# A two-layer 3x3 convolution with group norm: from 64x64 tiles on overlapping bands, two images at a time, to dense blocks of 16 rows by 8 channels, one image at a time, in 64x32 and 32x32 tiles

## The chip, the cores and the metric

The kernel runs on one core of one Trainium2 chip, alone. The metric is the device time of one execution in microseconds; lower is better. All arithmetic is float32.

## The reference

```python
def _gn(v, G=4, eps=1e-5):
    g = v.reshape(B_, G, C_ // G, H_, W_)
    m = jnp.mean(g, axis=(2, 3, 4), keepdims=True)
    s = jnp.var(g, axis=(2, 3, 4), keepdims=True)
    return ((g - m) / jnp.sqrt(s + eps)).reshape(v.shape)

# x: (8, 8, 1024, 1024) float32; each conv is 3x3, 8 to 8 channels, stride 1, padding 1, plus bias
x = x + _L0_conv_ref(_gn(x), L0_conv_weight, L0_conv_bias)
x = x + _L1_conv_ref(_gn(x), L1_conv_weight, L1_conv_bias)
return x
```

Group norm is over 2 channels of one image (4 groups). One image is 33.5 MB and x is 268.4 MB, so nothing stays on the chip between the layers. The normalisation is folded into the weights (scaled by 1/std) and the bias, the border is padded with the mean, and the residual is an identity added to the middle tap. Layer 0's result goes to a tensor mid in device memory, in the order row, channel, column.

## The kernel before

**Windows.** The images go in four pairs. A window is one layer of one pair; eight windows run in the order L0 pair 0, L0 pair 1, L1 pair 0, L0 pair 2, L1 pair 1, L0 pair 3, L1 pair 2, L1 pair 3 (WINDOWS). Statistics of x for a later pair are taken while a window runs: 4 or 8 tiles of 1 MB per 8 units; the last three windows have none.

**Units.** A unit is 12 output rows of both images, as two bands: 8 input rows by 8 channels (64 partitions) make 6 output rows by 8 channels (48 columns of a 64-column tile). Neighbouring bands share 2 input rows. There are 85 units and a short last one in a window, 688 in all. `convolve` (matmul at L653) does a unit in two halves of 512 columns, three horizontal taps kw each, and for each of these six steps four matmuls of 64x64, one for each quarter of the array. In layer 0 every band's 8 rows are read from x; in layer 1 the rows of mid are read once and the shared rows are copied on chip, by POOL (L405) and by ACT (L508).

**Engines.** SP issues the statistics loads. ACT evicts (L465 both images in layer 0, L470 one band in layer 1) and then issues the loads of the unit 8 ahead (L479, L492). DVE takes statistics of x (L700) and mid (L710), and in layer 1 evicts the second band (L727). POOL issues the stores (L371, L385). x_tile has a ring of 8 units, out_tile one of 4, the accumulator conv two halves used in turn. TensorE waits only at fixed places ahead of the next unit: for its rows, halos and accumulator.

**Sums.** The mean and variance of the next window are combined by small 128x128 matmuls (L555, L564), DVE steps (L746 to L828) and bias matmuls (L583, L592), all put among the last units of the window, so that TensorE's stream goes on between them. Only before the first window do they stand alone.

## Time and profile before

| | |
|---|---|
| runs | 4156.16, 4156.9 and 4147.31 us, median 4156.16 |
| span of the profiled execution | 4141.6 us, first to last instruction |
| TensorE matmul | 89% busy, 33232 records |
| DVE, ACT, POOL | 49%, 43%, 33% busy |
| device memory | 895.64 MB read, 536.87 MB written |

The span leaves out what lies around it in a run, so the timed runs are a little longer. A busy TensorE in this table means that at least one matmul is in its modelled length, not that the array is full. Each float32 matmul of the program stands as two records.

### The profile page before, as it was taken

To read this page: it belongs to the slowest core of one execution; us is meant where nothing else is said; L and a number is where in the kernel's file an instruction comes from. 1 tells how busy PE (TensorE), PEld (TensorE's weight loads), DVE (VectorE), ACT (ScalarE), POOL (GpSimd) and SP (SyncE) were. 2 spreads that over 40 slices of the span, in tenths; PEclk is the share of its full clock that TensorE was granted. 3 is DMA by queue.
4 is the path that set the end of the run, shared out by engine and by line. 5 is a ranking of instruction groups with operands and counts; after the bars stand their busy time and mean duration, and the time that the engine had idled before them with its cause. 6 is when DMAs were issued, how large, how long until landed. Compare 5 with 4: busy or idle time off the path is not lost.

```text
span 4141.6 us, 88712 instructions
## 1 busy us (share of the span) xinstructions
PE 3666.7 (89%) x33232; PEld 1715.4 (41%) x33232; DVE 2025.6 (49%) x3110; ACT 1762.8 (43%) x1381; POOL 1360.0 (33%) x1829
## 2 busy tenths in 40 slices
PE   0087777898889999999888999999999999999999
PEld 0032222353334433354333443345444444566665
DVE  6866666665556344446656444444445322232222
ACT  0032222343334555543333555544443555555554
POOL 0011111121112555531111455552111455555555
PEclk9999998999999999999999999999999999999999
DMA  9989999999999999999999999999999999999997
GB/s 333 396 291 393 386 374 371 366 368 387 382 382 331 331 367 385 380 318 391 390 388 384 305 357 371 374 295 368 362 355 333 291 306 306 306 287 304 305 303 237
DMA packets 367109, 1435.04 MB, mean 346 GB/s; under 512 B 49888, under 2 KB 50016, under 8 KB 334176
## 3 DMA queue, kind: packets, MB, share of 16 engines
q10 hardware_dynamic: 176736, 627.30, 47.9%
q0 software_dynamic: 153344, 536.96, 34.5%
q1 hardware_dynamic: 36864, 268.45, 16.9%
q8 instruction: 119, 1.95, 0.2%
q14 instruction: 46, 0.38, 0.0%
HBM read 895.64 MB, written 536.87 MB: 346 GB/s over the span
## 4 chain that ended last, share of the span: by engine, by line
PE 56%; DMA 15%; ACTq 11%; issue 10%; DVE 5%; ACT 2%; DVEq 0%; POOL 0%; POOLq 0%; SPq 0%
PE conv L653 56%; DMA out_dram<-out_tile 12%; ACTq L479 11%; DMA stat_tile<-x_dram 2%; DVE bn_x L700 2%; ACT out_tile L465 1%; DVE bn_mid L710 1%; DMA mid_dram<-out_tile 1%; DVE out_tile L727 1%; DVE mv_mid L738 1%; DVEq L700 0%; DVE mv_x L732 0%; PE conv L555 0%; ACTq L461 0%; PE conv L583 0%
## 5 line engine op out<-in xcount | busy, mean ns | idle before, releaser
L653 PE MATMUL conv<-x_tile,wts 64*64 64x512 f32 x32832 | 3648.7, 598 | 235.5 <-ACT out_tile L465 140.4
L653 PEld LDWEIGHTS conv<-x_tile,wts 64*64 64x64 f32 x32832 | 1694.9, 134 | 2170.3 <-issue 2037.0
L465 ACT ACTIVATE out_tile<-conv,bias 128x1024 f32<-128x1024 f32 x688 | 728.6, 1110 | 1340.5 <-PE conv L653 791.1
L710 DVE BATCH_NORM_STATS2 bn_mid<-out_tile 128x512 f32 (+1 forms) x1376 | 849.3, 680 | 881.1 <-ACT out_tile L465 880.9
L727 DVE TENSOR_SCALAR out_tile<-conv,bias 128x1024 f32<-128x1024 f32 x340 | 436.4, 1284 | 1168.7 <-PE conv L653 856.7
L371 POOL DMA_DIRECT2D mid_dram<-out_tile x680 | 343.4, 507 | 1708.1 <-ACT out_tile L465 1641.4
L470 ACT ACTIVATE out_tile<-conv,bias 128x1024 f32<-128x1024 f32 x344 | 383.1, 1114 | 764.4 <-PE conv L653 505.6
L508 ACT ACTIVATE x_tile<-x_tile 16x2048 f32<-16x2048 f32 x340 | 648.6, 1908 | 44.9 <-issue 31.6
L700 DVE BATCH_NORM_STATS2 bn_x<-stat_tile 128x512 f32 (+1 forms) x1024 | 628.7, 678 | 45.6 <-DMA stat_tile<-x_dram 45.5
L405 POOL COPY x_tile<-x_tile 16x2048 f32<-16x2048 f32 x340 | 639.1, 1880 | 1.7
L385 POOL DMA_DIRECT2D out_dram<-out_tile x680 | 348.3, 514 | 823.7 <-DVE out_tile L727 758.8
L555 PE MATMUL conv<-share,average 128*128 128x8 f32 x32 | 5.5, 281 | 227.4 <-DVE share L746 222.3
L555 PEld LDWEIGHTS conv<-share,average 128*128 128x128 f32 x32 | 4.8, 215 | 233.3 <-issue 221.5
L396 POOL COPY x_tile<-pad 128x4 f32<-128x4 f32 x64 | 12.2, 198 | 173.2 <-DVE pad L821 172.1
L522 ACT ACTIVATE root<-var 128x8 f32<-128x8 f32 x8 | 1.7, 208 | 137.3 <-DVE var L790 137.2
L738 DVE BATCH_NORM_AGGREGATE mv_mid<-bn_mid 128x2 f32<-128x12 f32 (+1 forms) x24 | 40.1, 1698 | 0.0
L522 ACT ACT_TABLE_LOAD x1 | 1.3, 1283 | 84.5 <-issue 84.5
L732 DVE BATCH_NORM_AGGREGATE mv_x<-bn_x 128x2 f32<-128x192 f32 x32 | 29.9, 983 | 0.0
L335 POOL TENSOR_SCALAR own_group<-same_group 128x4 f32<-128x4 f32 x2 | 0.4, 188 | 44.0 <-DMA rows<-taps_dram 43.9
L379 POOL DMA_DIRECT2D out_dram<-out_tile x16 | 7.8, 495 | 13.4 <-ACT out_tile L470 13.4
L592 PEld LDWEIGHTS conv<-taken,band 64*64 64x64 f32 x144 | 7.2, 134 | 2.2 <-issue 2.2
L583 PE MATMUL conv<-taken,band 64*64 64x1 f32 x144 | 5.5, 208 | 2.7 <-DVE taken L818 2.7
(62 smaller groups left out, 114.5 us busy)
## 6 DMA issues: line engine op xcount, KB each, us to landing
x_tile<-x_dram ACTq DMA_DIRECT2D x680, 512.0 KB, 23.0
stat_tile<-x_dram SPq DMA_DIRECT2D x256, 1024.0 KB, 9.8
out_dram<-out_tile POOLq DMA_DIRECT2D x680, 384.0 KB, 7.8
mid_dram<-out_tile POOLq DMA_DIRECT2D x672, 384.0 KB, 9.3
x_tile<-mid_dram ACTq DMA_DIRECT2D x340, 640.0 KB, 6.4
x_tile<-mid_dram ACTq DMA_DIRECT2D x344, 128.0 KB, 8.5
mid_dram<-out_tile POOLq DMA_DIRECT2D x8, 416.0 KB, 10.0
x_tile<-x_dram ACTq DMA_DIRECT2D x8, 256.0 KB
```

The lines of the kernel that those rows point to most:

```text
L371: pool.dma_start(mid[win.image + i, bass.ds(unit.n * OUT_ROWS + (CH - extra), OUT_ROWS + extra), :], out_tile[VALID - extra:VALID + OUT_RO ...
L385: pool.dma_start(pair[:, bass.ds(row, ROWS_OUT), :], out_tile[VALID:VALID + OUT_ROWS, slot, band]) \
L405: pool.tensor_copy(x_tile[0:PAIR, unit.slot, :, 1:SIDE + 1], x_tile[HALF:HALF + PAIR, earlier.slot, :, 1:SIDE + 1]) \
L465: last = act.activation(out_tile[0:parts, slot, i], conv[0:parts, bank, i], ACT.Identity, bias=bias0[0:parts, win.parity, int(unit.last), ...
L470: last = act.activation(out_tile[:, slot, 0], conv[:, bank, 0], ACT.Identity, bias=bias1[:, win.parity, unit.kind:unit.kind + 1])
L479: act.dma_start(x_tile[:, slot, band, 1:SIDE + 1], rows.rearrange("n c r w -> (n c) r w")) \
L508: act.activation(x_tile[HALF + HALF // 2:HALF + HALF // 2 + PAIR, unit.slot, :, 1:SIDE + 1], x_tile[HALF // 2:HALF // 2 + PAIR, unit.slot, ...
L653: last = nc.tensor.matmul(to, weights, x_tile[HALF * half:HALF * (half + 1), slot, middle, c + kw:c + kw + BANK], start=(kw == 0), stop=(k ...
L700: last = dve.bn_stats(bn_x[:, bass.ds(t * STAT_PARTS + q, 1), :].rearrange("p a b -> p (a b)"), stat_tile[:, s, q * BANK:(q + 1) * BANK])
L710: last = dve.bn_stats(bn_mid[0:parts, unit.win.pair % 2, i, bass.ds(unit.n * 2 + h, 1), :] .rearrange("p a b -> p (a b)"), out_tile[0:part ...
L727: dve.tensor_scalar(out_tile[:, slot, 1], conv[:, bank, 1], bias1[:, win.parity, INNER:INNER + 1], None, ALU.add) \
L738: return dve.bn_aggr(mv_mid[:, region, i, :], bn_mid[:, of.pair % 2, i, first:end, :] .rearrange("p a b -> p (a b)"))
```

## The change

The bands go. A block is 16 rows by 8 channels of one image, 128 partitions with nothing twice; block b of x_tile holds input rows 16b+1 to 16b+16, so that the output rows 16b to 16b+15 need its 15 first rows, its last for the row below, and the last two rows of the block before. A unit is two blocks (32 rows), 32 units are a pass, and a pass is one layer of one image: 16 passes in the order image 0 layer 0, image 0 layer 1, image 1 layer 0 and so on. Output rows come in quarters of 4 rows by 8 channels (32 columns). Quarters 1 and 3 need rows of one half of the block alone: `whole`, a 64x32 matmul. Quarters 0 and 2 need 32 partitions of their own and 32 above: `split`, two 32x32 matmuls. In the second block of a unit the quarters are shifted by two column strips, so that the four whole tiles cover strips 1 and 3 and the eight split tiles strips 0 and 2. Eviction swaps the halves back (three ACT operations). The part above adds into the other column half's bank, and a wait (half_added) keeps the two halves of a unit's split tiles apart.

All loads are issued by SP, up to seven blocks ahead; all evictions are ACT's; POOL issues the stores. The sums of a pass stand between passes: `sums` on TensorE comes after the last convolution and before the next, and layer 1's need the statistics of all of mid. Statistics tiles of the next image (32) go along units 0 to 58, with two extra at units 31 and 33. TensorE runs in a loop over passes with a loop over trips of four units inside.

```diff
-ROWS_IN = 8
-ROWS_OUT = 6
-BANDS = 2
+BLOCKS = SIDE // ROWS
+UNITS = BLOCKS // 2
+TRIP = 4
+TRIPS = UNITS // TRIP
+SLOTS = 2 * TRIP
+PASSES = 2 * IMAGES
+RING = 4
+EVICTS = 3
+FREE = 6
+STAT_UNITS = sorted(list(range(0, 60, 2)) + [31, 33])
+STAT_AHEAD = 2
...
+    x_by_row = x.rearrange("n c h w -> h n c w")
+    out_by_row = out.rearrange("n c h w -> h n c w")
...
-        x_tile = sb("x_tile", [P, X_RING, BANDS, SIDE + 2])
+        x_tile = sb("x_tile", [P, SLOTS, SIDE + 2])
...
+            def load_block(layer, n, b):
+                first = ROWS * b + 1
+                rows = ROWS - 1 if b == BLOCKS - 1 else ROWS
+                sp.dma_start(x_tile[0:CH * rows, b % SLOTS, 1:SIDE + 1],
+                             rows_of(layer, n, first, rows)).then_inc(rows_loaded[b % SLOTS], 16)
...
+            def image(n, last_image):
+                for g in range(2 * UNITS):
+                    layer, u = divmod(g, UNITS)
+                    if not last_image:
+                        for i in stat_at(g):
+                            load_stat(n + 1, i, STATS * n + (STATS + i + 1 - STAT_SLOTS))
+                    sp.wait_ge(conv_done, units_through(n, g))
+                    sp.sem_inc(rows_wanted)
+                    if g == UNITS:
+                        for s in range(RING):
+                            sp.wait_ge(stored[s], stores_before(n, UNITS + s))
...
+                    if (g + TRIP - 1) % UNITS == UNITS - 1:
+                        load_last_pad(layer, n)
+                        load(TRIP, 0)
+                        sp.wait_ge(last_pad_loaded, 32 * n + 16 * (layer + 1))
+                        sp.sem_inc(rows_wanted)
+                        load(TRIP - 1, 1)
+                    else:
+                        load(TRIP - 1, 1)
+                        load(TRIP, 0)
...
+            def store(n, g, i):
...
+                pool.wait_ge(evicted, evicts_through(n, g, EVICTS if i else 1))
+                pool.sem_inc(results_seen)
+                pool.dma_start(to, out_tile[:, g % RING, i]).then_inc(stored[g % RING], 16)
...
+            def evict(n, g, first_image):
+                layer, u = divmod(g, UNITS)
+                slot, parity = g % RING, g % 2
+                act.wait_ge(conv_done, units_through(n, g))
+                if g >= RING or not first_image:
+                    act.wait_ge(stored[slot], stores_before(n, g))
...
+                act.activation(out_tile[:, slot, 0], conv[:, parity, 0], ACT.Identity,
+                               bias=bias[:, 0:1]).then_inc(evicted, 1)
+                act.activation(out_tile[HALF:P, slot, 1], conv[0:HALF, parity, 1], ACT.Identity,
+                               bias=bias[0:HALF, 0:1]).then_inc(evicted, 1)
+                act.activation(out_tile[0:HALF, slot, 1], conv[HALF:P, parity, 1], ACT.Identity,
+                               bias=bias[HALF:P, 0:1]).then_inc(evicted, 1)
...
+            def sums(p):
+                pe.wait_ge(evicted, EVICTS * UNITS * p + (FREE - EVICTS))
+                pe.wait_ge(mean_share, p + 1)
+                pe.sem_inc(unit_begun)
+                nc.tensor.matmul(conv[:, 0, 0, 0:GROUPS], average[:, :], share[:, :], start=True,
+                                 stop=True).then_inc(mean_summed, 1)
...
+            def columns_of(parity, i, quarter, c):
+                column = TILE * ((quarter + 2 * i) % 4)
+                return conv[column:column + TILE, parity, i, c * BANK:(c + 1) * BANK]
+
+            def whole(parity, j, c, kw):
+                for i in range(2):
+                    for h in range(2):
+                        part = slice(HALF * h, HALF * (h + 1))
+                        nc.tensor.matmul(columns_of(parity, i, 2 * h + 1, c), wts[part, WHOLE, kw],
+                                         rows_of(HALF * h, HALF, 2 * j + i, c, kw),
+                                         start=(kw == 0), stop=(kw == KW - 1))
+
+            def split(parity, j, c, kw):
+                first, end = c == 0 and kw == 0, c == 1 and kw == KW - 1
+                for i in range(2):
+                    slot = 2 * j + i
+                    for h in range(2):
+                        part = slice(HALF * h, HALF * h + TILE)
+                        nc.tensor.matmul(columns_of(parity, i, 2 * h, c), wts[part, SPLIT, kw],
+                                         rows_of(HALF * h, TILE, slot, c, kw), start=first, stop=end)
+                        q = 1 if h else 3
+                        part = slice(TILE * q, TILE * (q + 1))
+                        above = slot if h else (slot - 1) % SLOTS
+                        last = nc.tensor.matmul(columns_of(parity, i, 2 * h, 1 - c),
+                                                wts[part, SPLIT, kw],
+                                                rows_of(TILE * q, TILE, above, 1 - c, kw),
+                                                start=first, stop=end)
+                return last
+
+            def convolve(p, t, j):
+                parity = j % 2
+                for i in range(2):
+                    pe.wait_ge(rows_loaded[2 * j + i], 16 * (TRIPS * p + t) + 16)
+                pe.wait_ge(evicted, EVICTS * (UNITS * p + TRIP * t) + (EVICTS * (j - 1) + FREE))
+                pe.sem_inc(unit_begun)
+                whole(parity, j, 0, 0)
+                split(parity, j, 0, 0)
+                whole(parity, j, 0, 1)
+                split(parity, j, 0, 1)
+                whole(parity, j, 0, 2)
+                split(parity, j, 0, 2).then_inc(half_added, 1)
+                whole(parity, j, 1, 0)
+                pe.wait_ge(half_added, UNITS * p + TRIP * t + (j + 1))
+                pe.sem_inc(unit_begun)
+                split(parity, j, 1, 0)
+                whole(parity, j, 1, 1)
+                split(parity, j, 1, 1)
+                whole(parity, j, 1, 2)
+                last = split(parity, j, 1, 2)
+                last.then_inc(conv_done, 1)
...
+            with pe.Fori(0, PASSES) as p:
+                sums(p)
+                pe.wait_ge(pads_written, p + 1)
+                pe.wait_ge(wts_ready, p + 1)
+                pe.sem_inc(unit_begun)
+                with pe.Fori(0, TRIPS) as t:
+                    for j in range(TRIP):
+                        convolve(p, t, j)
...
+            def take_mid(n, u):
+                for i in range(2):
+                    dve.wait_ge(evicted, evicts_through(n, u, EVICTS if i else 1))
+                    for h in range(HALVES):
+                        last = dve.bn_stats(bn_mid[:, (2 * u + i) * HALVES + h, :],
+                                            out_tile[:, u % RING, i, h * BANK:(h + 1) * BANK])
+                last.then_inc(mid_taken, 1)
...
+            def write_pads(p):
+                part = slice(P - TILE, P)
+                dve.tensor_tensor(above[:, :], own_mean[:, :], is_above[:, :], ALU.mult)
+                dve.tensor_scalar(x_tile[:, :, 0:SIDE + 2:SIDE + 1], ones[:, :, :],
+                                  own_mean[:, 0:1], None, ALU.mult)
...
+                dve.wait_ge(head_loaded, 16 * (p + 1))
+                dve.tensor_scalar(x_tile[part, LAST_SLOT, 1:SIDE + 1], head[part, :],
+                                  is_first[part, 0:1], above[part, 0:1], ALU.mult, ALU.add) \
+                   .then_inc(pads_written, 1)
...
+            def sums_of(n, layer):
+                p = 2 * n + layer
+                mean_shares(layer)
+                var_shares(p, layer)
+                variance(p)
+                make_weights(p, layer)
+                write_pads(p)
+                make_bias(p, layer)
+
+            def image(n, last_image):
+                begun[0] = FOR_IMAGE * n + AT_START
+                steps[0] = 0
+                dve.wait_ge(stat_used, STATS * n + STATS)
+                dve.sem_inc(sums_begun)
+                sums_of(n, 0)
+                for g in range(2 * UNITS):
+                    if g == UNITS:
+                        dve.wait_ge(mid_taken, UNITS * n + UNITS)
+                        dve.sem_inc(sums_begun)
+                        sums_of(n, 1)
+                    if g < UNITS:
+                        take_mid(n, g)
```

## Rows read from the trace of the kernel before

**Rows 1.** The page: engines over the span, and bytes moved.

```profile
PE 3666.7 (89%) x33232; PEld 1715.4 (41%) x33232; DVE 2025.6 (49%) x3110; ACT 1762.8 (43%) x1381; POOL 1360.0 (33%) x1829
...
DMA packets 367109, 1435.04 MB, mean 346 GB/s; under 512 B 49888, under 2 KB 50016, under 8 KB 334176
```

**Rows 2.** Stretches: length, busy us of each engine, clock, DMA share, GB/s.

```profile
100.00:200.00 100.00, 0.00 (x0) 0.00 (x0) 86.63 (x142) 0.00 (x0) 0.00 (x0) 1.00 1.01 391
300.00:800.00 500.00, 396.42 (x3252) 143.93 (x3248) 317.80 (x533) 142.57 (x136) 68.58 (x136) 0.92 1.02 379
1400.00:1700.00 300.00, 283.31 (x2612) 117.44 (x2610) 133.56 (x162) 163.18 (x108) 155.63 (x162) 1.00 1.02 374
1900.00:2200.00 300.00, 265.20 (x2368) 105.95 (x2364) 179.58 (x297) 103.79 (x98) 49.53 (x98) 0.98 1.03 387
2800.00:3100.00 300.00, 300.00 (x2800) 148.24 (x2798) 143.40 (x232) 123.88 (x118) 59.19 (x119) 1.00 1.01 364
3700.00:4100.00 400.00, 400.00 (x3728) 271.56 (x3726) 100.16 (x78) 235.41 (x156) 225.07 (x237) 1.00 0.99 304
```

**Rows 3.** Waits from 1900 to 2200 us: total, times, longest.

```profile
PE conv L653 <- ACT out_tile L465: 27.9, 13, 3.2
```

**Rows 4.** The DMA view of 1900 to 2200 us.

```profile
GB/s 409 404 383 383 399 303 394 400 388 409 407 386 350 404 393 371 401 407 336 394 405 400 407 407 383 374 392 399 410 404 347 397 396 372 352 407 398 346 409 368
...
q0 software_dynamic: 11001, 38.59, 33.1%
```

**Rows 5.** The DMA view of 2800 to 3100 us, ACT's queue.

```profile
q10 hardware_dynamic: 17296, 62.98, 61.9%
```

**Rows 6.** Groups by line and form over the whole span.

```profile
L653 PE MATMUL conv<-x_tile,wts 64*64 64x512 f32 x32832 | 3648.7, 598 | 235.5 <-ACT out_tile L465 140.4 <-DMA x_tile<-x_dram 41.5 <-DVE out_tile L727 39.3
...
L465 ACT ACTIVATE out_tile<-conv,bias 128x1024 f32<-128x1024 f32 x680 | 720.2, 1110 | 1334.2 <-PE conv L653 784.8 <-issue 481.1 <-DMA mid_dram<-out_tile 45.0
...
L710 DVE BATCH_NORM_STATS2 bn_mid<-out_tile 128x512 f32 x896 | 553.4, 680 | 560.1 <-ACT out_tile L465 559.9
...
L738 DVE BATCH_NORM_AGGREGATE mv_mid<-bn_mid 128x2 f32<-128x1020 f32 x8 | 37.9, 4743 | 0.0
...
L465 ACT ACTIVATE out_tile<-conv,bias 64x1024 f32<-64x1024 f32 x8 | 8.4, 1102 | 6.2 <-PE conv L653 6.2
```

**Rows 7.** Timeline around 3640 us: start, length, what.

```profile
3638.08 1.99 PE L653 MATMUL conv<-x_tile,wts 64*64 64x512 f32 x16
...
3640.00 0.74 PEld L555 LDWEIGHTS conv<-share,average 128*128 128x128 f32 x6 [0.81 <-issue]
...
3640.77 0.21 PEld L653 LDWEIGHTS conv<-x_tile,wts 64*64 64x64 f32 x8
3640.77 1.52 PE L653 MATMUL conv<-x_tile,wts 64*64 64x512 f32 x12
3641.25 0.15 PEld L653 LDWEIGHTS conv<-x_tile,wts 64*64 64x64 f32 x4 [0.28 <-issue]
```

**Rows 8.** Timeline of TensorE's matmuls around the bias sums.

```profile
804.33 0.99 PE L583 MATMUL conv<-taken,band 64*64 64x1 f32 x32
805.15 0.64 PE L653 MATMUL conv<-x_tile,wts 64*64 64x512 f32 x1
805.16 0.22 PE L583 MATMUL conv<-taken,band 64*64 64x1 f32 x2
```

**Rows 9.** Timeline of the sums before the first window.

```profile
211.46 7.18 DVE L732 BATCH_NORM_AGGREGATE mv_x<-bn_x 128x2 f32<-128x192 f32 x8
...
220.38 0.17 DVE L746 COPY share<-mv_x 128x8 f32<-128x8 f32 x1
...
220.70 0.57 PE L555 MATMUL conv<-share,average 128*128 128x8 f32 x2 [220.70 <-DVE share L746]
...
228.06 1.98 PE L653 MATMUL conv<-x_tile,wts 64*64 64x512 f32 x8 [0.68 <-DVE bias L846]
```

More of the change, by code:

```diff
@@ L289, in _, with rows_of @@
[L289 to L295 removed]
+            def rows_of(layer, n, first, rows):
+                if layer == 0:
+                    return x_by_row[first:first + rows, bass.ds(n, 1)].rearrange("r n c w -> r (n c) w")
+                return mid[bass.ds(n, 1), CH * first:CH * (first + rows), :] \
+                    .rearrange("n a w -> (n a) w")
@@ L307, in _ @@
+            pool.memset(is_above[:, :], 0.0)
             pool.memset(average[:, :], 1.0 / P)
@@ new lines, in image @@
+            def image(n, first_image):
+                for layer in range(2):
+                    act.wait_ge(var_read, 2 * n + (layer + 1))
+                    act.activation(root[:, :], var[:, :], ACT.Sqrt).then_inc(root_done, 1)
+                    act.wait_ge(wts_ready, 2 * n + (layer + 1))
+                    for u in range(UNITS):
+                        evict(n, layer * UNITS + u, first_image)
+            image(0, True)
+            with act.Fori(1, IMAGES) as n:
+                image(n, False)
@@ L560, in var_sum @@
-            def var_sum(n, bank):
-                pe.wait_ge(var_share, n + 1)
-                regions = 1 if WINDOWS[n].layer == 0 else 3
-                for region in range(regions):
-                    last = nc.tensor.matmul(conv[:, bank, 1, BANK:BANK + BOTH], average[:, :],
-                                            share[:, region], start=(region == 0),
-                                            stop=(region == regions - 1))
-                last.then_inc(var_summed, 1)
-            def own(i):
-                return slice(VALID * i, VALID * i + HALF)
```

927 lines of the change are left out of this document (249 added, 678 removed).

## Prediction

> **What bounds the kernel now.** I read the page's totals first [rows 1]: TensorE is busy 89% of the 4141.6 us span, and 1435 MB move at a mean of 346 GB/s. Both are averages over unlike stages, so the table by stretches comes next [rows 2], and it shows two regimes. From 3700 to 4100 us (layer 1 without statistics) TensorE never rests: 3728 matmul records in 400 us. A float32 matmul of the program leaves two records (16416 in the source, 32832 in the trace), and four 64x64 tiles run side by side, so a set of four records takes 400/932 = 0.429 us and a set of four program matmuls 0.858 us. The whole kernel has 4104 such sets, 3521 us: that is TensorE's floor. The stretches 300 to 800, 1400 to 1700 and 1900 to 2200 us are otherwise: TensorE is 79 to 94% busy while the DMA engines' share stands at 1.02 to 1.03 and the rate at 374 to 387 GB/s. The share alone proves nothing (it is 0.99 at 304 GB/s too, where nothing waits for a load), but here TensorE stands waiting for evictions [rows 3], whose engine also issues the loads and is held up. The DMA's view of 1900 to 2200 us [rows 4] has single slices of 7.5 us at 407 to 410 GB/s beside a mean of 387; the mean of those three stretches, weighted by length, is 380 GB/s. So the first half is bound by bytes, the last third by TensorE.
>
> **The change, part by part.**
>
> *Bytes.* The 8-rows-in, 6-rows-out bands and their 33% of repeated input go. Each of the five streams (statistics of x, load of x, store and load of mid, store of out) is now 268.4 MB, 1342 MB together instead of 1435. No halo copies are left on ACT or POOL. What shrinks is only 93 MB, some 245 us at 380 GB/s; the rest of any gain must come from lifting TensorE's floor.
>
> *TensorE.* A unit is now 32 rows of one image: 6 rounds (two column halves, three kw) of 4 whole (64x32) and 8 split (32x32) matmuls. Whole tiles take column strips 1 and 3, split tiles strips 0 and 2, over all rows, so the twelve fill the array exactly. If they overlap as the four do now, a round is 0.858 us and a unit 5.15 us. The wait for half_added in mid-unit costs the split strips one drain and one semaphore: a record lasts 0.60 us on average [rows 6] against 0.43 of streaming, 0.17 us, plus 0.15 us, the time from DVE's end at 220.55 to the first 128x128 matmul at 220.70 [rows 9]. I take 5.45 us, 512 units, 2790 us. Does that overlap hold? The trace has no 64x32 or 32x32 tile. The lower bound is 5.15 us. The upper bound is no overlap of the two shapes: four whole (0.858 us), then eight split (0.858 us), twelve phases in a unit, and at each switch what the trace shows where 64x64 gives way to 128x128 at 3640 us [rows 7]: the last set of the sixteen records starts 3 x 0.43 us after 3638.08, with its four members spread over 0.1 us, and streams until 3639.9, the weights of the other shape start only at 3640.00 (inside the stream they are loaded ahead), and on return the second set's weights come 0.48 us after the first's instead of 0.43: 0.09 + 0.05 = 0.14 us a switch. That is 12 x 1.00 = 12.0 us a unit. I take the lower bound, because the tiles conflict there (128x128 needs every strip) and here no two of the twelve share one, and because at 805 us [rows 8] records of the next block start before the last of the bias sums that precede them in the program: tiles wait for their own strip, not for the stream.
> The Trainium skill, TensorEngine Tiling (Array Packing), Key Properties, speaks against this: "Changing tiling mode (not just tile) drains the TensorE". The rows at 3640 us agree as far as they go, for 128x128 against 64x64; whether 64x32 against 32x32 is such a switch no row shows. By that rule every phase would be drained, which is the first rival below.
>
> *Feeding TensorE.* A round is 24 pairs of weight load and matmul where a set of four was 8. Hidden if a pair costs under 0.858/24 = 36 ns. The steady stream only shows 107 ns a pair (8 in 0.858 us); the bias sums' burst is 32 pairs in 0.99 us, less the last one's own length of about 0.2 us, 25 to 31 ns [rows 8]. Bounds 25 and 107; I take 28, hidden, since the burst is paced by 64-column weight loads and these have 32 columns.
>
> *ACT and DVE.* ACT evicts alone: three activations, 1.10 to 1.11 us each whether 128 or 64 partitions [rows 6], 3.3 us a unit. DVE has four statistics of 0.68 us in layer 0 and two more on average for the next image, 4.1 us. Both lie under the 6.9 us that the DMA needs for a unit (below). POOL issues two stores, about 1 us. SP now issues all loads, so that a load no longer sits behind an eviction, but only seven blocks run ahead.
>
> *DMA rate.* A unit with half a statistics tile is 2.62 MB: 6.9 us at 380 GB/s, against 5.45 us of TensorE. So the DMA becomes the bound nearly throughout. Bounds of its rate: 364 (2800 to 3100 us, x loads beside mid stores) and 396, halfway between the initial pure loads' 391 [rows 2] and the slices' 400 and more [rows 4]. I take 380, the mean of stretches with the same mix.
>
> *Pass boundaries.* Before, sums for the next window were hidden in the last units; now they stand between passes. Layer 0 to 1: last eviction 3.3, its statistics 1.4, the aggregate over 768 values 3.6 (4.74 x 768/1020, [rows 6]), then the chain of sums, root, weights and bias, 220.38 to 228.06 = 7.7 us [rows 9], plus about 1.3 us for writing pads and the 1024-wide top row (an operation of that width is 1.11 on ACT): 17.3 us. Layer 1 to 0: DVE has aggregated already, 9 us. Over 8 images TensorE stands 8 x 17.3 + 7 x 9 = 201 us. The DMA keeps working: at the last conv_done some 5 or 6 blocks, two units' stores and one or two statistics tiles are outstanding, 6 to 8 MB, 16 to 20 us, and new loads come 5.45 us after TensorE resumes. Idle DMA: 17.3 + 5.45 - 17 = about 6 us at each of 8, nothing at the others: 48 us (all exposed it would be near 250).
>
> *Start and end.* Before, 64 statistics tiles and 8 units of x, 75.5 MB, led to the aggregates at 211.5 us [rows 9]. Now 37.2 MB: 38.3 MB less at 391 GB/s is 98 us, so 114; aggregates for 4 groups instead of 8, 3.6 us; the chain, 9 us: TensorE starts at about 127. For the last eviction (3.3 us) and the landing of its stores I allow 8 us.
>
> *Sum.* 130 (start) + (1342 - 37 - 2)/0.380 = 3429 + 48 + 8 = 3615 us, against the profiled span of 4141.6. The timed runs, 4147 to 4157 with a median of 4156, lie 6 to 15 us above that span; I add 14 and say 3630.
>
> **Rivals.**
>
> *The two tile shapes don't overlap (slower; the change does not do what it says).* Place: each switch from whole to split and back, 12 in a unit. Price 12.0 us a unit, 6144 us, plus 127 + 201 + 8: 6480 us span; without any switch cost 12 x 0.858 = 10.3 us, 5610. For it: weights of another shape were not loaded ahead at 3640 us. Against it: disjoint strips, and the starts at 805 us [rows 8]. It decides from 7.4 us a unit: (4142 - 127 - 201 - 8)/512. The rule of the Trainium skill (TensorEngine Tiling (Array Packing), Key Properties) would give this rival.
>
> *TensorE is fed too slowly.* 144 pairs a unit; at 51 ns a pair the gain is gone (7.4/144), at 107 ns it is 15.4 us a unit and 8.2 ms. For it: no row shows a steady stream under 107. Against it: the burst near 28. A middle value of 60 ns gives 8.6 us a unit, 4760 us.
>
> *The new row order slows DMA.* Neighbouring partitions of x and out are now neighbouring channels, 4 MiB apart in memory, where they were consecutive rows of 16 planes. For it: loads of x occupy their queue at 62.98 MB per 61.9% of 300 us, 339 GB/s at full share [rows 5], stores of mid at 389 (38.59 MB per 33.1%) [rows 4]. If all 537 MB of x loads and out stores run at 339 and the rest at 390, the 3429 becomes 3553, 3740 us in all: still faster. It loses only under (1303 MB)/(4142 - 186) = 329 GB/s on average.
> The Trainium skill, DMA: Bandwidth & Descriptors, section Latency and other measured facts, gives 103 GB/s for a partition pitch of 4 MiB. By an estimate from that page, 537 MB would take 5.2 ms alone. The trace does not agree for the present loads, which already start in planes 4 MiB apart and run inside stretches of 364 to 387 GB/s.
>
> *DMA gains nothing because boundaries are exposed.* All 250 us open and 364 GB/s: 3580 + 130 + 250 + 8, 3970 us, still 4% faster.
>
> **How the numbers follow.** Forecast (shapes overlap, DMA-bound, 3480 to 3980 us) 0.58; shapes don't overlap 0.28; fed too slowly 0.08, about half of it ending slower; row order below break-even 0.03; something else 0.03. About 0.3% is what a measurement of this kernel can tell from no change. Faster 0.61, same 0.03, slower 0.36. The likeliest's own range is 3480 (1303 MB at 396 GB/s, 3290 + 186) to 3980; to leave out no more than 2 in 10 it must reach over the first rival, 3480 to 6560.
>
> **What would show it.** Right: the DMA share near 1 and 370 to 395 GB/s in every pass with statistics, TensorE's records in groups of twelve per 0.43 us where it runs unhindered, waits of TensorE on loads or evictions, 1342 MB in total, gaps of TensorE near 17 and 9 us alternating. Wrong: TensorE at 100% with units of 10 to 12 us and 220 to 260 GB/s (shapes don't overlap); units of 7 us or more with evenly spaced record starts (feeding); load packets that take longer in layer 0 than in layer 1 (row order); gaps much over 17 us.

## The result, and the profile after

The changed kernel takes 6540.48 us (median of four runs, 6538.91 to 6541.13) against 4156.53 us: 1.574 times as long (interval 1.571 to 1.578). The forecast, 3630 us and faster, was wrong in size and in direction. The first rival, that the two tile shapes don't overlap, had given 6480 us and a chance of 0.28; the wide range, 3480 to 6560 us, holds the measured time only because it was drawn over that rival.

The page of the changed kernel, totals, chain and groups, answers to [rows 1, 6]:

```profile
PE 6236.9 (95%) x74176; PEld 1052.5 (16%) x74176; DVE 1424.5 (22%) x2460; ACT 1711.8 (26%) x1553; POOL 591.4 (9%) x1059
...
DMA packets 334159, 1344.60 MB, mean 206 GB/s; under 512 B 38800, under 2 KB 38928, under 8 KB 301200
...
PE conv L395 47%; PE conv L405 45%; PE conv L410 3%; DMA stat_tile<-x_dram 1%; DVE bn_x L602 1%; DVE mv_mid L490 0%; ACT out_tile L344 0%; ACT out_tile L346 0%; DVE wts L541 0%; DVE bn_mid L476 0%; DVE newton L531 0%; DVE x_tile L556 0%; PE conv L371 0%; PE conv L367 0%; SPq L183 0%
...
L405 PEld LDWEIGHTS conv<-x_tile,wts 32*32 32x32 f32 x24576 | 530.4, 103 | 2591.3 <-issue 2591.3
L395 PEld LDWEIGHTS conv<-x_tile,wts 64*32 64x32 f32 x24576 | 475.9, 105 | 2612.3 <-issue 2612.3
```

L395 is the whole tile (64x32), L405 and L410 are the split tiles (32x32). The chain that ended last lies on TensorE for 95% of the span, and is shared evenly between L395 and L405: the two shapes take turns. The page counts 805.45 MB read and 536.87 MB written, the 1342 MB predicted; with the small packets they flow at 206 GB/s. The most telling rows are the last two: the weight loads of each shape stand idle for 2.6 ms with nothing that they wait for. Inside a stream of one shape they are loaded under the running matmuls; here the first load of each phase comes only when the other shape has ended.

The table by stretches, in the columns of [rows 2], says the same for the steady state:

```profile
3000.00:3300.00 300.00, 300.00 (x3588) 49.85 (x3592) 31.03 (x49) 83.23 (x75) 25.68 (x49) 1.00 0.62 211
```

TensorE is busy for 300 of 300 us at the full clock, but leaves 3588 records there, 12.0 per us. Twelve tiles in a full array would leave 12 per 0.43 us, 28 per us. "Busy" means only that at least one matmul is in its length.

The timeline of the changed kernel's matmuls shows a round: start, length, what (of each eight split records one or two stand here):

```profile
3000.00 0.61 PE L410 MATMUL conv<-x_tile,wts 32*32 32x512 f32 x1
...
3000.45 0.59 PE L405 MATMUL conv<-x_tile,wts 32*32 32x512 f32 x1
...
3000.49 0.59 PE L410 MATMUL conv<-x_tile,wts 32*32 32x512 f32 x1
3001.01 1.06 PE L395 MATMUL conv<-x_tile,wts 64*32 64x512 f32 x8
3002.00 0.61 PE L405 MATMUL conv<-x_tile,wts 32*32 32x512 f32 x1
```

and of its weight loads:

```profile
3001.01 0.15 PEld L395 LDWEIGHTS conv<-x_tile,wts 64*32 64x32 f32 x8 [0.84 <-issue]
3002.00 0.10 PEld L405 LDWEIGHTS conv<-x_tile,wts 32*32 32x32 f32 x1 [0.84 <-issue]
```

A phase is two sets of records 0.45 us apart and lasts 0.99 to 1.01 us, whichever shape. In the stretch shown L395 never starts between two split sets, though its column strips are free. This is the pattern of [rows 7], where 64x64 gives way to 128x128, twelve times a unit. Evictions of one unit and the next start 12.06 us apart (600.55 and 612.61 us). The sign written down for this rival was 10 to 12 us a unit at 220 to 260 GB/s.

The pass boundary from layer 0 to layer 1, the timeline of all engines:

```profile
508.09 1.11 ACT L342 ACTIVATE out_tile<-conv,bias 128x1024 f32<-128x1024 f32 x1 [8.68 <-PE conv L410]
...
511.50 1.29 DVE L476 BATCH_NORM_STATS2 bn_mid<-out_tile 128x6 f32<-128x512 f32 x2 [0.98 <-ACT out_tile L346]
...
512.95 3.62 DVE L490 BATCH_NORM_AGGREGATE mv_mid<-bn_mid 128x2 f32<-128x768 f32 x1 [0.15 <-DVE bn_mid L476]
...
525.75 1.93 PE L395 MATMUL conv<-x_tile,wts 64*32 64x512 f32 x8 [2.51 <-DVE bias L562]
```

From the first eviction to TensorE's return are 17.7 us. The sum there is another matter than the tiles, and it was predicted well (17.3): evictions 3.4, statistics 1.45, aggregate 3.62, the rest 9.2. From layer 1 to layer 0 of the next image it is 8.3 us (914.21 to 922.48), where 9 was said.

### The profile page after: what moved, and what is told of

It reads as the page before. It is cut to its first block, busy times and chain, and to the rows that moved or that the text cites. A ratio compares the mean times of both kernels' runs of the same rounds, so it can differ in the third digit from the quotient of the medians.

```text
span 6539.5 us, 167994 instructions
## 1 busy us (share of the span) xinstructions
PE 6236.9 (95%) x74176; PEld 1052.5 (16%) x74176; DVE 1424.5 (22%) x2460; ACT 1711.8 (26%) x1553; POOL 591.4 (9%) x1059
## 3 DMA queue, kind: packets, MB, share of 16 engines
q0 software_dynamic: 147456, 536.94, 21.9%
HBM read 805.45 MB, written 536.87 MB: 205 GB/s over the span
## 4 chain that ended last, share of the span: by engine, by line
PE 95%; DVE 2%; issue 1%; DMA 1%; ACT 1%; SPq 0%; DVEq 0%; ACTq 0%; POOL 0%; POOLq 0%
PE conv L395 47%; PE conv L405 45%; PE conv L410 3%; DMA stat_tile<-x_dram 1%; DVE bn_x L602 1%; DVE mv_mid L490 0%; ACT out_tile L344 0%; ACT out_tile L346 0%; DVE wts L541 0%; DVE bn_mid L476 0%; DVE newton L531 0%; DVE x_tile L556 0%; PE conv L371 0%; PE conv L367 0%; SPq L183 0%
## 5 line engine op out<-in xcount | busy, mean ns | idle before, releaser
L410 PE MATMUL conv<-x_tile,wts 32*32 32x512 f32 x24576 | 3334.1, 602 | 0.0
L405 PE MATMUL conv<-x_tile,wts 32*32 32x512 f32 x24576 | 3334.0, 602 | 0.0
L395 PE MATMUL conv<-x_tile,wts 64*32 64x512 f32 x24576 | 3281.4, 604 | 34.9 <-DVE bias L562 34.9
L342 ACT ACTIVATE out_tile<-conv,bias 128x1024 f32<-128x1024 f32 x512 | 570.6, 1114 | 4619.3 <-PE conv L410 4619.3
L476 DVE BATCH_NORM_STATS2 bn_mid<-out_tile 128x6 f32<-128x512 f32 x1024 | 658.7, 685 | 2241.6 <-ACT out_tile L342 1989.6
L468 DVE BATCH_NORM_STATS2 bn_x<-stat_tile 128x6 f32<-128x512 f32 x896 | 550.6, 679 | 2013.8 <-DMA stat_tile<-x_dram 2013.8
L405 PEld LDWEIGHTS conv<-x_tile,wts 32*32 32x32 f32 x24576 | 530.4, 103 | 2591.3 <-issue 2591.3
L395 PEld LDWEIGHTS conv<-x_tile,wts 64*32 64x32 f32 x24576 | 475.9, 105 | 2612.3 <-issue 2612.3
L346 ACT ACTIVATE out_tile<-conv,bias 64x1024 f32<-64x1024 f32 x512 | 569.3, 1112 | 13.1
L344 ACT ACTIVATE out_tile<-conv,bias 64x1024 f32<-64x1024 f32 x512 | 567.4, 1108 | 13.0
L297 POOL DMA_DIRECT2D out_dram<-out_tile x512 | 269.0, 525 | 2895.0 <-ACT out_tile L342 2425.9
L410 PEld LDWEIGHTS conv<-x_tile,wts 32*32 32x32 f32 x24576 | 530.4, 103 | 0.0
L602 DVE BATCH_NORM_STATS2 bn_x<-stat_tile 128x512 f32 x128 | 78.9, 681 | 24.1 <-DMA stat_tile<-x_dram 23.7
```

The source lines that it names most:

```text
L297: pool.dma_start(to, out_tile[:, g % RING, i]).then_inc(stored[g % RING], 16)
L342: act.activation(out_tile[:, slot, 0], conv[:, parity, 0], ACT.Identity, bias=bias[:, 0:1]).then_inc(evicted, 1)
L344: act.activation(out_tile[HALF:P, slot, 1], conv[0:HALF, parity, 1], ACT.Identity, bias=bias[0:HALF, 0:1]).then_inc(evicted, 1)
L346: act.activation(out_tile[0:HALF, slot, 1], conv[HALF:P, parity, 1], ACT.Identity, bias=bias[HALF:P, 0:1]).then_inc(evicted, 1)
L395: nc.tensor.matmul(columns_of(parity, i, 2 * h + 1, c), wts[part, WHOLE, kw], rows_of(HALF * h, HALF, 2 * j + i, c, kw), start=(kw == 0), ...
L405: nc.tensor.matmul(columns_of(parity, i, 2 * h, c), wts[part, SPLIT, kw], rows_of(HALF * h, TILE, slot, c, kw), start=first, stop=end)
```

## Experiments

The theories at the start: (A) any change of tile shape empties the array, wherever the tiles lie, at about 0.14 us and with no overlap across it; (B) TensorE can't take pairs of weight load and matmul fast enough; (C) DMA, evictions or the loop hold it back. Each kernel below is the changed one with the edit shown, if nothing else is said. A variant with the split tiles alone gave no time, since it reads parts of the accumulator that nothing writes.

### One shape only

```diff
 def whole(parity, j, c, kw):
+    first, end = c == 0 and kw == 0, c == 1 and kw == KW - 1
     for i in range(2):
         for h in range(2):
-            part = slice(HALF * h, HALF * (h + 1))
-            nc.tensor.matmul(columns_of(parity, i, 2 * h + 1, c), wts[part, WHOLE, kw],
-                             rows_of(HALF * h, HALF, 2 * j + i, c, kw),
-                             start=(kw == 0), stop=(kw == KW - 1))
+            for lower in range(2):
+                at = HALF * h + TILE * lower
+                side = 1 - c if lower else c
+                nc.tensor.matmul(columns_of(parity, i, 2 * h + 1, side),
+                                 wts[at:at + TILE, WHOLE, kw],
+                                 rows_of(at, TILE, 2 * j + i, side, kw),
+                                 start=first, stop=end)
...
-                whole(parity, j, 1, 0)
                 pe.wait_ge(half_added, UNITS * p + TRIP * t + (j + 1))
                 pe.sem_inc(unit_begun)
+                whole(parity, j, 1, 0)
```

> Every 64x32 whole matmul becomes two 32x32 ones, so the array has one tile shape, 16 tiles a round, and the program has more matmuls (96 instead of 72 a unit, 192 load-matmul pairs instead of 144). Theory A (a change of tile shape drains the array): rounds fall from 2.01 us to about 0.86 us, a unit to 5.15 + 0.3 us (all strips now wait at half_added), the DMA becomes the bound and the time is about 3640 us, 3500 to 4000. Rival B (what costs is the number of instructions: 12.05 us / 144 = 84 ns a pair): 192 pairs make 16.1 us a unit, 8500 us. Rival C (shapes don't matter; strips of whole and split work get in each other's way): unchanged near 6500 us.

Measured: 4011.88 us, 0.966 (0.964 to 0.968) of the kernel before. With 98752 records instead of 74176, a third more, the kernel is 2529 us faster. That decides against (B) as the cause of the 12.06 us. The size was missed, though: 3500 to 4000 us was expected, with 5.45 us a unit. Its timeline, matmuls:

```profile
2999.97 0.89 PE L398 MATMUL conv<-x_tile,wts 32*32 32x512 f32 x8
3000.26 0.61 PE L409 MATMUL conv<-x_tile,wts 32*32 32x512 f32 x1
...
3000.40 0.89 PE L398 MATMUL conv<-x_tile,wts 32*32 32x512 f32 x8
```

The lines of the former whole tiles (now L398) and of the split ones are interleaved, and the sets overlap. Two evictions of its layer 1, where nothing else holds it:

```profile
912.58 1.11 ACT L342 ACTIVATE out_tile<-conv,bias 128x1024 f32<-128x1024 f32 x1 [3.26 <-PE conv L414]
919.31 1.11 ACT L342 ACTIVATE out_tile<-conv,bias 128x1024 f32<-128x1024 f32 x1 [3.34 <-PE conv L414]
```

A unit is 6.7 us, for the same work that takes 12.06 us in two shapes. Within it, every second set of the split records (the first of eight stands here):

```profile
917.05 0.61 PE L409 MATMUL conv<-x_tile,wts 32*32 32x512 f32 x1
918.11 0.61 PE L409 MATMUL conv<-x_tile,wts 32*32 32x512 f32 x1
919.17 0.61 PE L409 MATMUL conv<-x_tile,wts 32*32 32x512 f32 x1
```

Two sets of sixteen take 1.06 us, 0.53 each, where 0.43 was expected; only the first sets after a stop come at 0.43. Twelve sets of 0.53 and the mid-unit wait of 0.3 (the split sets are 0.92 us apart there, from 921.74 to 922.65 us, where the slower step is 0.61 elsewhere) are the 6.7 us. Sixteen pairs of weight load and matmul in 0.53 us are 33 ns a pair: here feeding does cost, 0.10 us a set. That it is feeding is inferred from these figures; no run varied it alone.

### Fewer switches

```diff
                 whole(parity, j, 0, 0)
-                split(parity, j, 0, 0)
                 whole(parity, j, 0, 1)
-                split(parity, j, 0, 1)
                 whole(parity, j, 0, 2)
+                split(parity, j, 0, 0)
+                split(parity, j, 0, 1)
                 split(parity, j, 0, 2).then_inc(half_added, 1)
```

and the second half in the same way: 4 switches a unit in place of 12, the matmuls the same.

> Same matmuls, but in each column half all three whole steps come first and then all three split steps: 4 changes of shape in a unit instead of 12. Theory A: 8 changes x 0.145 us x 512 units = 594 us less, about 5950 us, with phases of 0.858 us and still no overlap between the shapes. Rival B: unchanged, 6540 us. If the shapes could overlap in longer groups: well under 5900 us.

Measured: 5939.2 us, 1.430 (1.426 to 1.433), as theory (A) had it (5950). Its timeline:

```profile
3001.18 2.78 PE L395 MATMUL conv<-x_tile,wts 64*32 64x512 f32 x24
3003.89 0.61 PE L405 MATMUL conv<-x_tile,wts 32*32 32x512 f32 x1
```

A phase of 24 records takes 2.71 us: six sets of 0.43, 2.57, and 0.14. (6540 - 5939)/(8 x 512) gives 0.147 us a switch. The switch itself is the smaller part; the lost overlap, twelve phases of 0.858 us of streaming where six would do, remains.

### The same records with one shape

```diff
-                part = slice(HALF * h, HALF * (h + 1))
+                part = slice(HALF * h, HALF * h + TILE)
                 nc.tensor.matmul(columns_of(parity, i, 2 * h + 1, c), wts[part, WHOLE, kw],
-                                 rows_of(HALF * h, HALF, 2 * j + i, c, kw),
+                                 rows_of(HALF * h, TILE, 2 * j + i, c, kw),
```

Quarters 1 and 3 get the products of only half of their rows; everything else, the count of instructions too, is as in the changed kernel. This one is called the half-product kernel below.

> Each whole matmul reads only the upper 32 of its 64 partitions, so it is 32x32 at the same place in the array; count, order, strips and banks of all matmuls stay as in the changed kernel. It leaves out half of the products of quarters 1 and 3. Theory A: the only difference is that no change of shape is left, so the drains go: rounds of 0.858 us, DMA-bound, 3640 us (3500 to 4000). Rival B (instruction count) and rival C (order or strips): unchanged, 6540 us.

Measured: 3873.33 us, 0.932 (0.929 to 0.935), with 74176 records as in the changed kernel. The one thing that differs is the height of a third of the tiles, and 2667 us go. Count, order, loop, evictions and DMA transfers are the same, so neither (B) nor (C) can be the cause of the 12.06 us. The timeline in its last pass:

```profile
3799.76 0.63 PE L395 MATMUL conv<-x_tile,wts 32*32 32x512 f32 x4
3799.83 0.59 PE L410 MATMUL conv<-x_tile,wts 32*32 32x512 f32 x1
...
3800.19 0.63 PE L395 MATMUL conv<-x_tile,wts 32*32 32x512 f32 x4
```

Twelve records per 0.43 us, L395 among the others: just the overlap that the forecast had taken for granted. Evictions are 5.7 us apart (3753.65 and 3759.37 us), 6.3 at every fourth unit, where the loop turns; the forecast said 5.45. This run is the DMA-bound case of the forecast made real, and its stretches (columns of [rows 2]) test the rest of the sum:

```profile
612.00:832.00 220.00, 189.22 (x4271) 98.53 (x4262) 112.67 (x180) 99.35 (x90) 31.98 (x60) 0.95 0.99 360
832.00:862.00 30.00, 14.17 (x278) 8.18 (x263) 19.39 (x40) 4.84 (x6) 3.97 (x3) 0.66 0.40 160
867.00:1062.00 195.00, 180.12 (x4243) 94.19 (x4232) 38.45 (x61) 99.31 (x90) 31.29 (x60) 1.00 1.00 390
1062.00:1085.00 23.00, 14.30 (x311) 8.44 (x291) 4.75 (x24) 5.27 (x6) 4.04 (x4) 0.78 0.68 246
3690.00:3860.00 170.00, 169.11 (x4148) 99.81 (x4126) 0.00 (x0) 96.75 (x88) 30.39 (x58) 1.00 0.98 347
```

Layer 0 moves 360 GB/s, layer 1 390, and the DMA is idle at the boundary 0 to 1 for 30 x 0.60 = 18 us and at 1 to 0 for 23 x 0.32 = 7.4 us.

### Does it matter which side of the tile changes, and where it lies?

Two kernels made from the kernel before, whose four 64x64 tiles have a quarter of the array each. In the middle tap, one matmul of each pair gets 32 columns (it leaves out half of that tap's outputs there; the weights and the place of the output are cut to the same 32 columns, not shown):

```diff
+                                if middle and kw == 1:
+                                    column = HALF * (band if win.layer == 0 else i)
+                                    part = slice(column, column + HALF // 2)
...
```

> The kernel before with one third of its matmuls touched: for the middle tap the second matmul of each pair uses 32 of its 64 columns (it leaves out the middle tap's products for half of the output channels and rows of that band). 64x64 and 64x32 alternate, with the same rows. If any change of tile shape drains the array: each such set of four (1368 of 4104) falls into four phases of about 1.0 us instead of one of 0.858, 3.1 us more each, about 8450 us. If only a change in the number of rows does: 4150 us, unchanged.

or 32 rows (it leaves out half of that tap's inputs there):

```diff
+                                rows = HALF // 2 if middle and kw == 1 else HALF
                                 last = nc.tensor.matmul(
-                                    to, weights,
-                                    x_tile[HALF * half:HALF * (half + 1), slot, middle,
+                                    to, weights[0:rows],
+                                    x_tile[HALF * half:HALF * half + rows, slot, middle,
```

> The kernel before, for the middle tap the second matmul of each pair reads 32 of its 64 partitions (it leaves out their products). 64x64 and 32x64 alternate, with the same columns. If a change in rows drains the array, as the 64x32 and 32x32 tiles of the changed kernel suggest: about 8450 us. If the drain belongs only to disjoint strips or to something in the changed kernel: 4150 us.

Measured: 8018.63 us with mixed columns and 9795.91 us with mixed rows, one run each. Both compute less than the kernel before and take 1.9 and 2.3 times as long. Some 8450 us was expected of either if every change of shape drains the array, 4150 us if it doesn't. The weight loads with mixed columns:

```profile
7004.20 0.13 PEld L666 LDWEIGHTS conv<-x_tile,wts 64*32 64x32 f32 x2 [0.81 <-issue]
7005.17 0.19 PEld L666 LDWEIGHTS conv<-x_tile,wts 64*64 64x64 f32 x2 [0.84 <-issue]
7006.17 0.14 PEld L666 LDWEIGHTS conv<-x_tile,wts 64*32 64x32 f32 x2 [0.81 <-issue]
7007.14 0.21 PEld L666 LDWEIGHTS conv<-x_tile,wts 64*64 64x64 f32 x8 [0.84 <-issue]
```

and with mixed rows:

```profile
7000.79 0.19 PEld L654 LDWEIGHTS conv<-x_tile,wts 32*64 32x64 f32 x2 [0.81 <-issue]
7002.16 0.30 PEld L654 LDWEIGHTS conv<-x_tile,wts 64*64 64x64 f32 x8 [1.18 <-issue]
...
7006.16 0.19 PEld L654 LDWEIGHTS conv<-x_tile,wts 32*64 32x64 f32 x2 [0.81 <-issue]
7007.16 0.19 PEld L654 LDWEIGHTS conv<-x_tile,wts 64*64 64x64 f32 x2 [0.81 <-issue]
```

Each single matmul of a mixed set (two records, 0.858 us) now stands alone and takes 0.97 to 1.00 us with its switch. A mixed set then takes some 3.1 us more, and the floor of 3521 us becomes 3521 + 1368 x 3.1 = 7762; the page of the kernel with mixed columns has TensorE busy for 7781. The 8450 us had added the 3.1 us to a time in which TensorE also waited. Narrowing the columns alone is enough, and so is narrowing the rows, and in neither do two tiles share a part of the array. Theory (A) holds in its broad form. What sets the two apart is the clock, told under the hardware below: from 3000 to 3400 us the kernel with mixed columns leaves 1721 records at a granted clock of 1.00, the one with mixed rows 1384 at 0.82.

### Would a deeper loop win back the boundaries?

The all-32x32 kernel with `TRIP = 8`: sixteen slots of x instead of eight, fifteen blocks ahead instead of seven, and a loop body of eight units.

> The all-32x32 kernel with 16 slots of x_tile instead of 8 (trips of 8 units), so 15 blocks instead of 7 can be loaded ahead over a pass boundary. In the all-32x32 run a unit never took under 6.7 us, layer 0 passes averaged 7.5 us and boundary intervals were 27 and 18 to 19 us. If the loads that run ahead are what was missing at the boundaries: units stay near 6.7 us throughout, 512 x 6.7 + 8 x (20 + 12) + 130 = 3820 us. If they are not: 4010 us, unchanged.

Measured: 5413.74 us, 1.295 (1.293 to 1.298). The expectation fell: 1402 us slower than with `TRIP = 4`. The whole run's queue of instruction loads, and a stop of TensorE near 3000 us:

```profile
q8 instruction: 894, 14.65, 1.1%
```

```profile
3005.98 0.59 PE L409 MATMUL conv<-x_tile,wts 32*32 32x512 f32 x1
3009.79 0.61 PE L414 MATMUL conv<-x_tile,wts 32*32 32x512 f32 x1 [3.22 <-issue]
```

TensorE stops in the middle of a set with nothing to wait for, and 894 packets of 16 KB on the queue of instructions stand where the same kernel with `TRIP = 4` had 6. Units are between 6.7 us and some 20 us, the long ones every eighth. Such stops of TensorE, which end with no event that the profile shows, are 797 us in all (at L398, L409 and L414), the longest on split tiles 4.2 us; how the rest of the 1402 us divides between the lower granted clock (0.905 against 0.967) and the shorter gaps was not worked out. So a fourth theory: (D) the body is too long to stay near the engine and is read again each time the loop turns. (894 - 6) packets over 64 trips are 14 a trip.

The half-product kernel of above with `TRIP = 8`, a shorter body (2304 weight loads and matmuls against 3072), which leaves out the same products:

> The run in which whole matmuls read 32 of 64 partitions (half of the products of quarters 1 and 3 left out), with 16 slots instead of 8. With one shape and unhindered units of 5.7 us it took 3873 us where the sum said 3615 + 14. If the missing 240 us are DMA time lost at boundaries because only seven blocks run ahead: 3650 to 3750 us. If the DMA's rate in mid-pass was overrated: 3850 us, little changed.

Measured: 4446.45 us (one run), 573 us more than with `TRIP = 4`, where 3650 to 3850 was expected; the stops of the same kind are 576 us. Its queue:

```profile
q8 instruction: 702, 11.50, 1.1%
```

11 packets a trip. Theory (D) then says that a body of 1536 should run without stops at either depth of prefetch. Two kernels leave out a third tap as well, beside the products of above, with `TRIP = 4` (the second half of the unit is cut in the same way, and each sum ends at the second tap):

```diff
                 whole(parity, j, 0, 1)
-                split(parity, j, 0, 1)
-                whole(parity, j, 0, 2)
-                split(parity, j, 0, 2).then_inc(half_added, 1)
+                split(parity, j, 0, 1).then_inc(half_added, 1)
```

> The same with 8 slots, beside the run before it: how much running ahead is worth when TensorE has time. If boundaries with idle DMA are what the 8-slot kernels lose: about 3820 us, 100 to 170 us above the 16-slot run. If not, equal.

and with `TRIP = 8`:

> From the run with whole matmuls on 32 of 64 partitions: the third tap is left out as well (a third of the matmuls), with 16 slots. Its trip body of 8 units has 1536 TensorE records, as many as the body of 4 units in the all-32x32 run, which was not held up; the 16-slot runs had 2304 and 3072 and stood still for 1 to 2.4 us at times. If those stops are the reading of a loop body that is too long: no stops here, DMA-bound, 3650 to 3750 us. If 16 slots themselves hurt: over 4200 us.

Measured: 3766.07 us and 3665.11 us (one run each), both near what was expected. The instruction queue of the deep one has 6 packets again. Where the body fits, the deeper loop, with its prefetch, is worth 101 us; where it doesn't, it costs 573 or 1402. Sixteen slots alone are not what hurts, since the deep kernel with two taps has them too. Stretches of the shallow one and of the deep one:

```profile
3000.00:3300.00 300.00, 207.42 (x3920) 94.57 (x3900) 118.67 (x200) 133.44 (x121) 45.08 (x81) 0.85 0.96 364
```

```profile
3000.00:3300.00 300.00, 206.04 (x4072) 97.62 (x4084) 102.53 (x178) 140.18 (x127) 47.21 (x86) 0.85 0.96 375
```

14 and 11 packets of 16 KB a trip are some 230 and 180 KB, and those bodies stop; half of the one and two thirds of the other, 115 to 120 KB by this estimate, don't. No run lies between 120 and 180 KB. The Trainium skill (Advanced Engine Details and Errata, ISA Cache) gives TensorE an instruction cache of 128 KB in lines of 16 KB, and the runs agree with that: packets of 16 KB, and a limit between 120 and 180 KB. The packets name no engine; that they are TensorE's is inferred from its idle time and from the count, which goes with its body.

### The best full version

The all-32x32 kernel waits once in mid-unit for all sixteen tiles. Here strips 1 and 3 go on at the first of two signals, meant to come from the last record of the former whole tiles. `whole` is as in that kernel, and the lines are against the changed one:

```diff
-                whole(parity, j, 0, 2)
+                whole(parity, j, 0, 2).then_inc(half_added, 1)
                 split(parity, j, 0, 2).then_inc(half_added, 1)
+                pe.wait_ge(half_added, 2 * UNITS * p + 2 * TRIP * t + (2 * j + 1))
+                pe.sem_inc(unit_begun)
                 whole(parity, j, 1, 0)
-                pe.wait_ge(half_added, UNITS * p + TRIP * t + (j + 1))
+                pe.wait_ge(half_added, 2 * UNITS * p + 2 * TRIP * t + (2 * j + 2))
```

> The all-32x32 kernel (8 slots) with the mid-unit wait in two parts: strips 1 and 3 resume when their own last tiles of the first half have ended, strips 0 and 2 at the second signal, where before all sixteen tiles waited for the last of them. The all-32x32 run had units of 6.7 us, of which one set started 0.74 us after the one before it instead of about 0.2 us after its last member. If that wait is exposed: 0.1 to 0.3 us less a unit in the passes that TensorE bounds, 20 to 100 us less, 3910 to 3990 us. If the first signal comes too late to help: 4010 us.

Measured: 3999.43 us (3992.78 to 4004.03), 0.960 (0.957 to 0.963) of the kernel before, and the fastest that computes everything, by a small step: the all-32x32 kernel had 4011.88 us and 0.966. A unit of layer 1 takes 6.6 us instead of 6.7 (evictions at 915.16 and 921.75 us). That lies between the two expectations, 3910 to 3990 us if the wait was exposed and 4010 if not. TensorE takes 6.9 us at every fourth unit, the loop's turn, and in layer 0 it still waits for loads of x (97.9 us in all).

## Why the prediction was wrong

**What bound the kernel before**: nothing that ran speaks against it. The all-32x32 kernel, with 6% fewer bytes and a TensorE unit of 6.7 us, under the break-even of 7.4, came out 3.4% faster.

**The step that failed** is in the part on TensorE: "I take the lower bound, because the tiles conflict there (128x128 needs every strip) and here no two of the twelve share one, and because at 805 us [rows 8] records of the next block start before the last of the bias sums that precede them in the program: tiles wait for their own strip, not for the stream." The second half of that is true only among tiles of one shape: the bias sums and the convolution of [rows 8] are both 64x64. It says nothing on 64x32 beside 32x32. The row that did bear on a change of shape was the one at 3640 us [rows 7], and it was set aside on an argument about geometry. The rule of the Trainium skill (TensorEngine Tiling (Array Packing), Key Properties), that a change of tiling mode and not just of tile drains the engine, was quoted and given 0.28. The traces agree with it: one shape 5.7 us a unit, two shapes 12.06 us, with the same number of records.

**The rival's numbers**: 1.00 us a phase, 0.14 us a switch, 12.0 us a unit, 6480 us. Measured 0.99 to 1.01, 0.147, 12.06, a span of 6539.5. What is missing: 512 x 0.06 = 31 us in the units. At the boundaries, eviction starts lie 32.0 and 22.3 us apart on average (540.28 - 508.09, 936.65 - 914.21 and so on; 12.06 of them the unit): 20.0 and 10.3 us, so 8 x 20.0 + 7 x 10.3 = 232 against 201. The gaps themselves were nearly right (17.7 against 17.3, 8.3 against 9); the rest, 2.0 to 2.5 us each time, is the clock after them. The table by stretches of the changed kernel:

```profile
508.00:525.00 17.00, 1.96 (x28) 1.79 (x28) 12.36 (x29) 3.54 (x4) 3.97 (x3) 0.56 0.50 185
526.00:540.00 14.00, 14.00 (x144) 1.93 (x136) 6.05 (x11) 0.00 (x0) 0.00 (x0) 0.84 0.00 0
```

After a gap in which TensorE was busy for 2 of 17 us, the clock is at 0.84 on average for the first unit: it begins at the lower level, 1.2 GHz (0.50 from 525.7 to 529 us), where eight records take 1.93 us in place of 1.06. The first convolution starts at 119.6 us instead of 127, but its unit is slower by 2.5 for the same reason, so 5 less; the end takes 10.2 us instead of 8. Together: 6480 + 31 + 31 - 5 + 2 = 6539.

**Feeding**: right that it is hidden with twelve tiles: twelve pairs came in 0.43 us (36 ns a pair) without a gap. The 28 ns taken for a pair was too low: sixteen pairs take 0.53 us in the all-32x32 kernel, 33 ns a pair, so the margin under the 36 was small. The mid-unit wait was sized at 0.3 us: that holds in the all-32x32 kernel. In the half-product kernel a unit is 5.7 us, 0.57 above 5.15, and the loop's turn at every fourth unit adds 0.6, which the sum didn't have.

**ACT, DVE**: right; 1.11 us an eviction of either height, 0.68 us a statistic, never the bound of the changed kernel. In the half-product kernel TensorE waits for evictions for 100 us in all (L342 28.5, L344 49.3, L346 21.9); what held these back was not followed.

**The DMA-bound sum** was too low by its own mechanism, too. The half-product kernel shows about what the forecast would have come to: a span of 3869 us against 3615. Idle DMA at the boundaries is 8 x 18 + 7 x 7.4 = 196 us instead of 48: in the 30 us around the boundary 0 to 1 the DMA moves 30 x 0.160 = 4.8 MB, new loads included, where a backlog of 6 to 8 MB alone was assumed. Layer 0 of the first seven images, some 590 MB, at 360 GB/s instead of 380 costs 590/0.360 - 590/0.380 = 86 us; layer 1, as much, at 390 gives back some 40; the last image, where TensorE is busy 150 of 150 us (3490 to 3640) and 169 of 170 and 357 and 347 GB/s flow, costs 28. That is 3615 + 148 + 86 - 40 + 28 = 3837, of 3869, although TensorE starts at 117 us, where the sum had 130 (and its own part on the start 127): some 45 us stay unplaced. The forecast's own range, 3480 to 3980, would have held this time, by its width and not because its terms were right.

**The row order of x** may be where layer 0 loses. The DMA's view of the half-product kernel, load queue, in the middle of layer 0:

```profile
q1 hardware_dynamic: 10936, 47.67, 61.9%
```

and in the middle of layer 1:

```profile
q1 hardware_dynamic: 10277, 44.72, 59.9%
```

47.67 MB in 61.9% of 220 us is 350 GB/s at full share, 44.72 MB in 59.9% of 195 us 383. Both also carry the statistics loads of x, about a third of their bytes. The last image has none; its layer 0 (3490 to 3640 us) and layer 1 (3690 to 3860 us):

```profile
q1 hardware_dynamic: 7331, 26.65, 56.6%
q1 hardware_dynamic: 7655, 27.84, 49.7%
```

That is 314 GB/s for x and 330 for mid. So loads of x are the slower ones, the direction that the rival named. They were at 339 before [rows 5], 8% above the 314, beside other transfers; whether the new order costs something stays open, as no run changes the order alone. The rate of the Trainium skill for a pitch of 4 MiB (DMA: Bandwidth & Descriptors, Latency and other measured facts), 103 GB/s, isn't borne out: loads of x come at 314, and the stores of out, in the same order, run inside the 390 GB/s of layer 1. The page measured rows of 16 KB a partition, longer than the 4 KB here, and no run here varied that.

**Boundaries exposed**: in part right, 196 of the 250 us, but without turning the result.

## What to carry to other kernels

In these runs tiles on disjoint parts of TensorE overlapped only if they had the same rows and the same columns. Cut everything to the smallest shape that is needed and pay for more instructions, since a third more of them in one shape beat the mix by 2529 us. When the trace holds one row about the very event that a plan depends on, and an argument from geometry says otherwise, the row deserves the greater chance. Before lengthening a hardware loop, count the instructions of its body, and look at the queue of instruction loads afterwards.

## What was unexpected of the hardware

- A change of tile shape costs 0.11 to 0.15 us and all overlap across it, by rows or by columns alone, for tiles that share no part of the array (12.06 against 5.7 us a unit; two records alone in 0.97 to 1.00 us).
- Among tiles of one shape records start out of program order: with all tiles 32x32, the first records of L409 (3000.26 us) start before the second ones of L398 (3000.40 us), which stand ahead of them.
- A loop body of 2304 or 3072 weight loads and matmuls is read again on every trip (702 and 894 packets of 16 KB), with stops up to 4.2 us in mid-unit; one of 1536 isn't (6 packets), whether it comes as four units or as eight.
- A TensorE that the table has as always busy can get the lower clock for a good part of the time. The kernel with mixed rows, a single 32-row matmul alone in many phases:

```profile
3000.00:3400.00 400.00, 400.00 (x1384) 92.84 (x1376) 72.91 (x89) 87.67 (x58) 83.75 (x87) 0.82 0.52 149
```

  The granted clock is 0.82. Two phases of two records, the columns as before:

```profile
7000.80:7002.20 1.40, 1.40 (x7) 0.22 (x6) 0.00 (x0) 0.00 (x0) 0.00 (x0) 0.70 0.00 0
7006.20:7007.20 1.00, 1.00 (x4) 0.19 (x3) 0.60 (x1) 0.22 (x1) 0.02 (x1) 1.00 0.28 90
```

  The first takes 1.37 us (7000.79 to 7002.16), the second, at the full level, 1.00 (7006.16 to 7007.16). With mixed columns the clock is 1.00 in the same stretch. The kernels with two taps, where TensorE rests a third of the time, get 0.85. What exactly the chip looks at these runs don't show.
